# Per-chunk casts and per-chunk input loads between FFN2 and the second layer norm (8 cores, sequence block with MoE)

## The chip, the cores and the metric

One Trainium2 chip, all 8 cores, each with its own sequence of 4096 tokens and no exchange between them. The metric is the device time in microseconds of the slowest core.

## The reference, cut to what matters

Each core has x of 4096 tokens x 1024 features. LN is a layer norm.

```
h  = LN(x) W_to ; a damped rotation is scanned over time ; h = out W_from
x2 = x + 0.1 h
x3 = x2 + 0.1 (gelu(LN(x2) W_ffn1 + b1) W_ffn2 + b2)
p1 = LN(x + x3)
final = sum over 8 experts of w[e] * (silu(gate) * up) down[e]^T ,  w from the top 2 of 8 router logits
out = LN(p1 + final)
```

## The kernel before

Everything is kept transposed, features on the partitions: a tile is 512 tokens (T), 1024 features are 8 chunks (KC) of 128 x 512, and a core walks over 8 tiles (NT). Float32 buffers X0 (the input x), X2 (the running sum) and ACC (the output sum) hold one tile each; BFIN0 and BFIN1 hold the bfloat16 operand of the matmuls, in turn by tile.

A tile passes these stages: LN3 of X2 (`emit_ln`, L685), FFN1 (`emit_ffn1`, L610, 256 matmuls of L625), FFN2 (`emit_ffn2`, L639), the second layer norm p1 (`emit_ln` with twopass, L691), the router (L699 to L732), the experts (L770 gate and up, L810 down). LN1, the scan and W_from of the next tile (`make_chain`) are woven into the experts of this one.

FFN2 has two halves, `fr` = 0 and 1, each for four output chunks. A half takes four slabs (`kr`) of 1 MB of w2, with 32 matmuls of 128x512 each (L658), summed in four PSUM banks that begin with a bias matmul (L655). When a bank is done, DVE makes X2 = X2 + 0.1 PB (L668) and u = X0 + X2, in place in X2 (L671). The u of chunks 0 to 3 comes at the end of the first half, that of 4 to 7 at the end of the second.

`emit_ln` casts the eight chunks to bfloat16 on ACT (L385), sums them over the partitions on PE with a matrix of ones (L390), squares them on ACT (L393), sums again (L398); DVE then makes mean and 1/sqrt (L403 to L411) and the normalised chunks (L418, L419).

The order of the work is written out by hand: every engine has one list of instructions, filled in the order in which the Python code calls `opi` and `opd`, and `w(engine, marks)` puts a wait on a semaphore into that list. Whatever stands behind a wait on an engine is held by it. All loads and stores are issued by SP ("sync"), so they share one list.

Weights come through RING, four slots of 1 MB. `emit_slab_load` (L360) takes the next slot, makes SP wait for the matmuls that last read it, and issues one load (L369) from a bfloat16 scratch copy in HBM (scr_w, scr_gu, scr_dp). In tile 0 the copy doesn't exist yet: `prepass_unit` (L248) loads a slab in float32 into two slots by eight DMAs (L257), casts the halves on DVE (L288) and ACT (L286) into a third slot, and stores that to the scratch (L292).

The input of the next tile is loaded into X0 by `emit_xload` (L307): one wait, then eight loads of 256 KB (L312). It is called behind FFN2:

```
if i + 1 < NT:
    emit_xload(i + 1, extra=u_ms[KC - 1])
```

The output of a tile is normalised and stored (L824 to L832) in the middle of the next tile's FFN1, behind its fourth slab.

Of the kernel before, what the change touches and what calls it, by code (L numbers as in the profile page):

```python
# [14 lines left out]
T = 512  # L15
NT = S // T
KC = D // 128
# [12 lines left out]
def build(stop_stage="full"):  # L30
# [28 lines left out]
    def sb(name, shape, dt=F32):  # L59
        return es.enter_context(nc.sbuf_tensor(name, shape, dt))  # L60
# [4 lines left out]
    with es:  # L65
        X0 = sb("X0", [128, KC * T])
# [50 lines left out]
        def w(eng, ms):  # L117
            if ms is None:
                return
            if isinstance(ms, list):  # L120
                for m in ms:
                    w(eng, m)
                return
            sk, v = ms
            q[eng].append(lambda E, s=sems[sk], vv=v: E.wait_ge(s, vv))
# [8 lines left out]
        def opi(eng, sk, fn):  # L134
            cnt[sk] += STEP[sk]
            v = cnt[sk]
            q[eng].append(lambda E, fn=fn, s=sems[sk], st=STEP[sk]: fn(E).then_inc(s, st))
            if eng in DRAIN_ENGS:
                q[eng].append(lambda E: E.drain())  # L139
            return (sk, v)  # L140

        def opd(eng, sk, fn):
            cnt[sk] += STEP[sk]
            v = cnt[sk]
            q[eng].append(lambda E, fn=fn, s=sems[sk], st=STEP[sk]: fn(E).then_inc(s, st))
            return (sk, v)
# [4 lines left out]
        def xc(buf, k, width=T):  # L151
            return buf[:, k * width:(k + 1) * width]
# [12 lines left out]
        def ring_set_free(j, ms):  # L165
            if isinstance(ring_free[j], list):
                ring_free[j] = ring_free[j] + [ms]
            else:
                ring_free[j] = ms
# [133 lines left out]
        xTr = xT.rearrange("(k p) t -> k p t", p=128)  # L303
        outTr = outT.rearrange("(k p) t -> k p t", p=128)
        x_ms = [None] * (NT + 1)

        def emit_xload(i, extra=None):  # L307
            t0 = i * T
            w("sync", extra)
            ms = None  # L310
            for k in range(KC):
                ms = opd("sync", "SX", lambda E, k=k, t0=t0: E.dma_start(out=xc(X0, k), in_=xTr[k, :, t0:t0 + T]))  # L312
            x_ms[i] = ms
# [46 lines left out]
        def emit_slab_load(dram_ap, key):  # L360
            if key not in scr_ready:
                srcs, dram = _scr_srcs(key)
                ms_cs, mw, jo, oslot = prepass_unit(srcs, dst_dram=dram)
                scr_ready[key] = mw
                ring_free[jo] = [mw]
                return jo, oslot, ms_cs
            jj, slot, msf = ring_slot()
            w("sync", msf)
            ms = slot_dma(jj, lambda E, d=slot, s=dram_ap: E.dma_start(out=d, in_=s))  # L369
            return jj, slot, ms  # L370
# [3 lines left out]
        def emit_ln(src, bfin_p, gv=None, bv=None, dstf=None, out_bf=True,  # L374
                    src_ready=None, extra_swait=None, extra_twait=None, extra_vwait=None,
                    twopass=False):
            BFIN = BFINS[bfin_p]
            w("scalar", src_ready)
            w("scalar", extra_swait)
            w("scalar", bfin_user[bfin_p])  # L380
            cast_ms = [None] * KC
            sq_ms = [None] * KC
            mmS_ms = [None] * KC
            for k in range(KC):
                cast_ms[k] = opi("scalar", "S", lambda E, k=k: E.activation(out=xc(BFIN, k), in_=src(k), func=AF.Copy))  # L385
            w("tensor", bank_free[0])
            w("tensor", extra_twait)
# [251 lines left out]
        def emit_ffn2(i, g_ms, u_ms):  # L639
            x3_ms = [None] * KC  # L640
            if i == 0:
                w("tensor", ms_b2c)
            for fr in range(2):
                for kr in range(4):
                    jj, slot, msl = emit_slab_load(scr_w2[fr * 4 + kr], ("w2", fr * 4 + kr))
                    w("tensor", msl)
                    for jx in range(8):
                        w("tensor", g_ms[kr * 8 + jx])
                    mm_last = None
                    for oc4 in range(4):  # L650
                        oc = fr * 4 + oc4
                        b = 2 + oc4
                        if kr == 0:
                            w("tensor", bank_free[b])
                            opi("tensor", "T", lambda E, b=b, oc=oc: E.matmul(  # L655
                                PB[b][:], B2R[0:1, oc * 128:(oc + 1) * 128], ONER[:], start=True, stop=False))
                        for jx in range(8):
                            mm_last = opi("tensor", "T", lambda E, jx=jx, kr=kr, oc4=oc4, b=b, slot=slot: E.matmul(  # L658
                                PB[b][:], slot[:, jx * 512 + oc4 * 128: jx * 512 + (oc4 + 1) * 128], xc(G, kr * 8 + jx),
                                start=False, stop=(kr == 3 and jx == 7)))  # L660
                        if kr == 3:
                            bank_ready[b] = mm_last
                    ring_set_free(jj, mm_last)
                for oc4 in range(4):
                    oc = fr * 4 + oc4
                    b = 2 + oc4
                    w("vector", bank_ready[b])
                    x3_ms[oc] = opi("vector", "V", lambda E, oc=oc, b=b: E.scalar_tensor_tensor(  # L668
                        out=xc(X2, oc), in0=PB[b][:], scalar=0.1, in1=xc(X2, oc), op0=OP.mult, op1=OP.add))
                    bank_free[b] = x3_ms[oc]  # L670
                    u_ms[oc] = opi("vector", "V", lambda E, oc=oc: E.tensor_tensor(  # L671
                        out=xc(X2, oc), in0=xc(X0, oc), in1=xc(X2, oc), op=OP.add))
            return x3_ms

        last_gu_mm = [None]
        prev_out_so = [None]
# [5 lines left out]
        for i in range(NT):  # L682
            t0 = i * T
            x2_last = st["x2_7"]
            ms_ln3, _, _, ln3_bf, _ = emit_ln(lambda k: xc(X2, k), i % 2, gv=G3V, bv=B3V, src_ready=x2_last)  # L685
            g_ms = emit_ffn1(i, ms_ln3, ln3_bf)
            u_ms = [None] * KC
            x3_ms = emit_ffn2(i, g_ms, u_ms)
            if i + 1 < NT:
                emit_xload(i + 1, extra=u_ms[KC - 1])  # L690
            ms_p1bf, ms_p1f, ms_p1sq, p1_bf, p1_f = emit_ln(lambda k: xc(X2, k), i % 2, dstf=lambda k: xc(ACC, k), out_bf=True,  # L691
                                                            src_ready=u_ms[KC - 1], extra_vwait=prev_out_so[0], twopass=True)
            st["x2_free"] = ms_p1sq
            BFIN = BFINS[i % 2]
            w("tensor", bank_free[6])
# [53 lines left out]
            for e in range(NE):  # L749
# [48 lines left out]
                for fr in range(2):  # L798
# [5 lines left out]
                    for oc4 in range(4):  # L804
                        oc = fr * 4 + oc4
# [18 lines left out]
            def make_p2(i=i, t0=t0, acc_ms=list(acc_ms), gu_ms=last_gu_mm[0]):  # L824
                def p2():
                    _, ms_out, _, _, _ = emit_ln(lambda k: xc(ACC, k), i % 2, dstf=lambda k: xc(ACC, k), out_bf=False,
                                                 src_ready=acc_ms[KC - 1], extra_swait=gu_ms)
                    w("sync", ms_out)
                    for k in range(KC):
                        opd("sync", "SO", lambda E, k=k, t0=t0: E.dma_start(out=outTr[k, :, t0:t0 + T], in_=xc(ACC, k)))  # L830
                    prev_out_so[0] = ("SO", cnt["SO"])
                return p2  # L832
# [21 lines left out]
def _get_nc(stop_stage):  # L854
    if stop_stage not in _CACHE:
        _CACHE[stop_stage] = build(stop_stage)
    return _CACHE[stop_stage]
# [37 lines left out]
```

## Time and profile before

| what | value |
|---|---|
| median of 2 runs | 5834.64 us |
| the two runs | 5725.51 and 5943.76 us |
| the profiled execution, its own time | 5557.22 us |
| its span, slowest core (core 1) | 5555.6 us |
| spans of all 8 cores | 5534.1 to 5555.6 us |
| mean granted TensorE clock | 0.871 to 0.876 of full |

The profile is one execution; its times are not those of the two runs, which both took longer. Busy times and starts are in us from the span's start. PE is TensorE, DVE VectorE, ACT ScalarE, POOL GpSimd; SPq is SP's queue that issues DMAs. A bracket at the end of a timeline row gives the engine's idle time before it and what released it.

### The profile page before, as it was taken

To read this page: it belongs to the slowest core of one execution; us is meant where nothing else is said; L and a number is where in the kernel's file an instruction comes from. 1 tells how busy PE (TensorE), PEld (TensorE's weight loads), DVE (VectorE), ACT (ScalarE), POOL (GpSimd) and SP (SyncE) were. 2 spreads that over 40 slices of the span, in tenths; PEclk is the share of its full clock that TensorE was granted. 3 is DMA by queue.
4 is the path that set the end of the run, shared out by engine and by line. 5 is a ranking of instruction groups with operands and counts; after the bars stand their busy time and mean duration, and the time that the engine had idled before them with its cause. 6 is when DMAs were issued, how large, how long until landed. Compare 5 with 4: busy or idle time off the path is not lost.

```text
span 5555.6 us, 55775 instructions; the slowest of 8 cores (5534.1 to 5555.6 us)
## 1 busy us (share of the span) xinstructions
PE 4182.1 (75%) x17824; PEld 1772.5 (32%) x17824; DVE 1982.1 (36%) x2879; ACT 1040.6 (19%) x1559; POOL 467.2 (8%) x391
## 2 busy tenths in 40 slices
PE   1475656657898678966898678976899678976897
PEld 0122222223343233422333233432344233432343
DVE  4313432232443235332443235332443235332333
ACT  1222212221201221121211221121201211121111
POOL 0001000000200011100201010100201010100210
PEclk6687788768999889988999789988999789988999
DMA  2275657624233223314333233414234233323342
GB/s 62 91 250 174 212 201 238 230 92 147 107 128 129 99 106 114 137 61 151 107 123 136 91 107 114 137 68 151 99 122 144 84 108 113 137 75 136 114 144 91
DMA packets 178009, 712.61 MB, mean 128 GB/s; under 512 B 28609, under 2 KB 28737, under 8 KB 112194
## 3 DMA queue, kind: packets, MB, share of 16 engines
q1 hardware_dynamic: 168770, 708.95, 36.6%
q8 instruction: 156, 2.56, 0.2%
q10 hardware_dynamic: 8960, 0.10, 0.1%
q14 instruction: 123, 1.01, 0.1%
HBM read 625.09 MB, written 83.89 MB: 128 GB/s over the span
## 4 chain that ended last, share of the span: by engine, by line
PE 62%; DVE 17%; DMA 6%; ACT 5%; SPq 5%; issue 3%; DVEq 1%; ACTq 1%
PE PB L770 27%; PE PB L810 15%; PE PB L625 8%; PE PB L658 7%; SPq L257 4%; DMA RING<-guT 3%; ACT RING L286 2%; DVE ZS L438 2%; DVE PB L411 1%; ACT BFIN L385 1%; PE PB L390 1%; DVE UPE L783 1%; PE PB L598 1%; DVEq L139 1%; DVE PRD L789 1%
## 5 line engine op out<-in xcount | busy, mean ns | idle before, releaser
L770 PE MATMUL PB<-BFIN,RING 128*128 128x512 bf16 x8192 | 1877.3, 392 | 173.1 <-ACT RING L286 116.0
L770 PEld LDWEIGHTS PB<-BFIN,RING 128*128 128x128 bf16 x8192 | 814.5, 100 | 1216.5 <-issue 329.1
L810 PE MATMUL PB<-PRD,RING 128*128 128x512 bf16 x4096 | 963.9, 398 | 225.6 <-DVE PRD L789 140.0
L625 PE MATMUL PB<-BFIN,RING 128*128 128x512 bf16 x2048 | 518.9, 416 | 424.5 <-DMA RING<-scr_w 220.8
L783 DVE TENSOR_TENSOR UPE<-PB,CBE 128x512 f32<-128x512 f32 x512 | 354.2, 692 | 1024.4 <-PE PB L770 994.6
L810 PEld LDWEIGHTS PB<-PRD,RING 128*128 128x128 bf16 x4096 | 410.6, 102 | 773.7 <-issue 350.7
L816 DVE TENSOR_TENSOR ACC<-PB,ACC 128x512 f32<-128x512 f32 x512 | 354.2, 692 | 682.7 <-PE PB L810 673.6
L789 POOL TENSOR_TENSOR PRD<-SG,UPE 128x512 bf16<-128x512 bf16 x256 | 297.0, 1160 | 2879.0 <-DVE UPE L783 2804.4
L777 ACT ACTIVATE SG<-PB 128x512 bf16<-128x512 f32 x512 | 303.7, 598 | 1023.6 <-PE PB L770 1015.0
L658 PE MATMUL PB<-G,RING 128*128 128x512 bf16 x2048 | 465.0, 386 | 24.5 <-issue 14.0
L625 PEld LDWEIGHTS PB<-BFIN,RING 128*128 128x128 bf16 x2048 | 213.0, 104 | 729.0 <-issue 539.5
L658 PEld LDWEIGHTS PB<-G,RING 128*128 128x128 bf16 x2048 | 197.2, 99 | 275.3 <-issue 56.1
L668 DVE SCALAR_TENSOR_TENSOR X<-PB,X 128x512 f32<-128x512 f32 x64 | 44.3, 692 | 651.1 <-PE PB L658 651.1
L427 POOL TENSOR_TENSOR ACC<-X,MEANT 128x512 f32<-128x512 f32 x64 | 82.9, 1296 | 2056.3 <-DVE BFIN L419 2056.3
L755 ACT ACTIVATE CBE<-PB 128x512 f32<-128x512 f32 x64 | 38.2, 597 | 1142.1 <-PE PB L752 1095.4
L631 ACT ACTIVATE G<-PB,BHV 128x512 bf16<-128x512 f32 x256 | 175.7, 687 | 280.6 <-PE PB L625 280.4
L789 DVE TENSOR_TENSOR PRD<-SG,UPE 128x512 bf16<-128x512 bf16 x256 | 187.4, 732 | 62.0 <-DVE UPE L783 61.4
L286 ACT ACTIVATE RING<-RING 128x2048 bf16<-128x2048 f32 x64 | 122.2, 1909 | 383.5 <-DMA RING<-dpT 165.0
L288 DVE CAST RING<-RING 128x2048 bf16<-128x2048 f32 x64 | 80.0, 1251 | 293.9 <-DMA RING<-guT 106.4
L385 ACT ACTIVATE BFIN<-X 128x512 bf16<-128x512 f32 x128 | 68.1, 616 | 480.2 <-DVE X L671 428.4
L390 PE MATMUL PB<-BFIN,ONESB 128*128 128x512 bf16 x192 | 74.2, 556 | 95.5 <-ACT BFIN L385 95.5
L403 DVE TENSOR_SCALAR MEANT<-PB 128x512 f32<-128x512 f32 x24 | 16.6, 691 | 357.5 <-PE PB L390 357.5
(120 smaller groups left out, 1837.7 us busy)
## 6 DMA issues: line engine op xcount, KB each, us to landing
RING<-scr_gu SPq DMA_DIRECT2D x224, 1024.0 KB, 4.9
RING<-scr_w SPq DMA_DIRECT2D x112, 1024.0 KB, 5.2
RING<-scr_dp SPq DMA_DIRECT2D x112, 1024.0 KB, 5.0
RING<-guT SPq DMA_DIRECT2D x256, 256.0 KB, 5.7
scr_gu<-RING SPq DMA_DIRECT2D x32, 1024.0 KB, 4.9
RING<-dpT SPq DMA_DIRECT2D x128, 256.0 KB, 5.3
X<-xT SPq DMA_DIRECT2D x64, 256.0 KB, 5.1
RING<-w1T SPq DMA_DIRECT2D x64, 256.0 KB, 6.2
```

The source lines that it names most:

```text
L257: ms_rd = slot_dma(jj, lambda E, d=slot.bitcast(F32)[:, gg * gc_:(gg + 1) * gc_], s=srcs[hv][gg]: E.dma_start(out=d, in_=s))
L286: ms_c = opi(eng, sk, lambda E, d=dstap, s=slot.bitcast(F32)[:, 0:ncols]: E.activation(out=d, in_=s, func=AF.Copy))
L390: mmS_ms[k] = opi("tensor", "T", lambda E, k=k: E.matmul(PB[0][:], ONESB[:], xc(BFIN, k), start=(k == 0), stop=(k == KC - 1)))
L625: mmm = opi("tensor", "T", lambda E, k=k, fc4=fc4, b=b, slot=slot: E.matmul(PB[b][:], slot[:, k * 512 + fc4 * 128: k * 512 + (fc4 + 1) * 1 ...
L631: g_ms[fc] = opi("scalar", "S", lambda E, b=b, fc=fc: E.activation(out=xc(G, fc), in_=PB[b][:], func=AF.Gelu, bias=BHV[:, fc:fc + 1]))
L658: mm_last = opi("tensor", "T", lambda E, jx=jx, kr=kr, oc4=oc4, b=b, slot=slot: E.matmul(PB[b][:], slot[:, jx * 512 + oc4 * 128: jx * 512 ...
L770: mmm = opi("tensor", "T", lambda E, k=k, fc4=fc4, b=b, slot=slot, BFIN=BFIN: E.matmul(PB[b][:], slot[:, k * 512 + fc4 * 128: k * 512 + (f ...
L777: sg_ms[gc] = opi("scalar", "S", lambda E, b=b, gc=gc: E.activation(out=xc(SG, gc), in_=PB[b][:], func=AF.Silu))
L783: ms_up = opi("vector", "V", lambda E, b=b, par=par: E.tensor_tensor(out=xc(UPE, par), in0=PB[b][:], in1=CBE[:], op=OP.mult))
L789: prev_upe[par] = opi(peng, psem, lambda E, uc=uc, par=par: E.tensor_tensor(out=xc(PRD, uc), in0=xc(SG, uc), in1=xc(UPE, par), op=OP.mult))
L810: mmm = opi("tensor", "T", lambda E, k=k, oc4=oc4, b=b, slot=slot: E.matmul(PB[b][:], slot[:, k * 512 + oc4 * 128: k * 512 + (oc4 + 1) * 1 ...
L816: acc_ms[oc] = opi("vector", "V", lambda E, oc=oc, b=b: E.tensor_tensor(out=xc(ACC, oc), in0=PB[b][:], in1=xc(ACC, oc), op=OP.add))
```

## The change

It does two things. `emit_ln` takes a list of eight marks as `src_ready` and puts one wait before each cast instead of one before all; the second layer norm passes the eight u marks. And the call of `emit_xload` behind FFN2 goes; `emit_ffn2` itself issues the load of one chunk of the next tile's x right behind the u of that chunk. The first call of `emit_ln` (LN3) and tile 0's first x load stay.

```
-            w("scalar", src_ready)
+            per_chunk = isinstance(src_ready, list) and len(src_ready) == KC
+            if not per_chunk:
+                w("scalar", src_ready)
...
             for k in range(KC):
+                if per_chunk:
+                    w("scalar", src_ready[k])
                 cast_ms[k] = opi("scalar", "S", ...)
...
                     u_ms[oc] = opi("vector", "V", lambda E, oc=oc: E.tensor_tensor(
                         out=xc(X2, oc), in0=xc(X0, oc), in1=xc(X2, oc), op=OP.add))
+                    if i + 1 < NT:
+                        w("sync", u_ms[oc])
+                        x_ms[i + 1] = opd("sync", "SX", lambda E, oc=oc, t1=(i + 1) * T: E.dma_start(
+                            out=xc(X0, oc), in_=xTr[oc, :, t1:t1 + T]))
...
-            if i + 1 < NT:
-                emit_xload(i + 1, extra=u_ms[KC - 1])
             ms_p1bf, ms_p1f, ms_p1sq, p1_bf, p1_f = emit_ln(...
-                                                            src_ready=u_ms[KC - 1], extra_vwait=prev_out_so[0], twopass=True)
+                                                            src_ready=u_ms, extra_vwait=prev_out_so[0], twopass=True)
```

SP's list from FFN1 to the first expert of a tile behind the first, before (scr_w1 and scr_w2 are the scratch copies of the FFN weights, scr_gu that of gate and up):

```order
L830 DMA outT<-ACC 128x512 x7
L369 DMA RING<-scr_w1 128x4096 [waits sem_T] x4
L369 DMA RING<-scr_w2 128x4096 [waits sem_T] x8
L312 DMA X0<-xT 128x512 [waits sem_V]
L312 DMA X0<-xT 128x512 x7
L369 DMA RING<-scr_gu 128x4096 [waits sem_T] x4
```

The same stretch of SP's list now:

```order
L836 DMA outT<-ACC 128x512 x7
L369 DMA RING<-scr_w1 128x4096 [waits sem_T] x4
L369 DMA RING<-scr_w2 128x4096 [waits sem_T] x4
L679 DMA X0<-xT 128x512 [waits sem_V] x4
L369 DMA RING<-scr_w2 128x4096 [waits sem_T] x4
L679 DMA X0<-xT 128x512 [waits sem_V] x4
L369 DMA RING<-scr_gu 128x4096 [waits sem_T] x4
```

Four x loads, each with a wait for DVE, have moved ahead of the last four w2 loads.

ACT's list behind FFN2 of tile 1, before (L385 are the casts, L393 the squares, L409 the square root):

```order
L385 ACTIVATE BFIN1<-X2 128x512 [waits sem_V,sem_T]
L385 ACTIVATE BFIN1<-X2 128x512 x7
L393 ACTIVATE BFIN1<-X2 128x512 [waits sem_T] x8
L409 ACTIVATE PB1<-PB1 128x512 [waits sem_V]
```

And now:

```order
L389 ACTIVATE BFIN1<-X2 128x512 [waits sem_T,sem_V]
L389 ACTIVATE BFIN1<-X2 128x512 [waits sem_V] x7
L397 ACTIVATE BFIN1<-X2 128x512 [waits sem_T] x8
L413 ACTIVATE PB1<-PB1 128x512 [waits sem_V]
```

No instruction has changed its place there; seven casts have a wait of their own.

## Rows read from the trace of the kernel before

**Rows 1.** The page's head and part 1: busy time, share, instructions.
```profile
span 5555.6 us, 55775 instructions; the slowest of 8 cores (5534.1 to 5555.6 us)
PE 4182.1 (75%) x17824; PEld 1772.5 (32%) x17824; DVE 1982.1 (36%) x2879; ACT 1040.6 (19%) x1559; POOL 467.2 (8%) x391
```

**Rows 2.** The page's part 4, the chain that ended last, by engine and line.
```profile
PE 62%; DVE 17%; DMA 6%; ACT 5%; SPq 5%; issue 3%; DVEq 1%; ACTq 1%
PE PB L770 27%; PE PB L810 15%; PE PB L625 8%; PE PB L658 7%; SPq L257 4%; DMA RING<-guT 3%; ACT RING L286 2%; DVE ZS L438 2%; DVE PB L411 1%; ACT BFIN L385 1%; PE PB L390 1%; DVE UPE L783 1%; PE PB L598 1%; DVEq L139 1%; DVE PRD L789 1%
```

**Rows 3.** Timeline (start, us, instruction), tile 3, end of FFN2 and second LN.
```profile
2605.29 0.69 DVE L671 TENSOR_TENSOR X<-X 128x512 f32<-128x512 f32 x1
2606.06 3.69 SPq L312 DMA_DIRECT2D X<-xT  x8
2606.13 4.26 ACT L385 ACTIVATE BFIN<-X 128x512 bf16<-128x512 f32 x8 [59.59 <-DVE X L671]
2610.54 3.57 PE L390 MATMUL PB<-BFIN,ONESB 128*128 128x512 bf16 x8 [6.14 <-ACT BFIN L385]
2613.91 2.48 PE L398 MATMUL PB<-BFIN,ONESB 128*128 128x512 bf16 x8
```

**Rows 4.** Timeline, tile 3, middle of FFN2.
```profile
2545.83 29.64 SPq L369 DMA_DIRECT2D RING<-scr_w  x5
...
2575.01 0.39 PE L655 MATMUL PB<-ONER,B2R 1*128 1x512 bf16 x1
...
2575.97 0.69 DVE L671 TENSOR_TENSOR X<-X 128x512 f32<-128x512 f32 x1
```

**Rows 5.** DMA issues (count, KB each, us to landing): 2553.0 to 2555.5, 2561 to 2562, 2575 to 2576.
```profile
RING<-scr_w SPq DMA_DIRECT2D x1, 1024.0 KB, 4.9
RING<-scr_w SPq DMA_DIRECT2D x1, 1024.0 KB, 5.3
RING<-scr_w SPq DMA_DIRECT2D x1, 1024.0 KB, 4.7
```

**Rows 6.** Timeline of PE and ACT, tile 4, sums of LN3.
```profile
3040.09 1.89 PE L390 MATMUL PB<-BFIN,ONESB 128*128 128x512 bf16 x8
3041.81 3.53 PE L398 MATMUL PB<-BFIN,ONESB 128*128 128x512 bf16 x8
```

**Rows 7.** Timeline, tile 3, FFN1 behind the output stores; landing of its first slab.
```profile
2505.64 4.45 SPq L830 DMA_DIRECT2D outT<-ACC  x8
2510.19 65.28 SPq L369 DMA_DIRECT2D RING<-scr_w  x12
2516.49 29.27 PE L625 MATMUL PB<-BFIN,RING 128*128 128x512 bf16 x128 [30.45 <-DMA RING<-scr_w]
...
RING<-scr_w SPq DMA_DIRECT2D x1, 1024.0 KB, 6.1
```

**Rows 8.** Windows: stretch, us, busy of each engine, PEclk, DMA share, GB/s.
```profile
2513.00:2516.50 3.50, 0.01 (x1) 0.04 (x2) 0.00 (x0) 0.00 (x0) 0.00 (x0) 0.50 1.02 396
2516.50:2519.00 2.50, 2.50 (x6) 0.83 (x7) 0.00 (x0) 0.00 (x0) 0.00 (x0) 0.50 1.03 341
2519.00:2522.00 3.00, 3.00 (x14) 1.37 (x13) 0.00 (x0) 2.05 (x3) 0.00 (x0) 0.91 0.99 407
2546.00:2575.00 29.00, 29.00 (x132) 12.48 (x131) 4.15 (x6) 0.54 (x1) 0.00 (x0) 1.00 0.41 145
2575.00:2604.00 29.00, 29.00 (x132) 12.57 (x132) 5.28 (x8) 0.00 (x0) 0.00 (x0) 1.00 0.11 37
2646.00:2700.00 54.00, 50.51 (x222) 21.67 (x221) 16.63 (x23) 14.89 (x26) 22.59 (x18) 0.97 0.31 107
```

**Rows 9.** Timeline of PE: after 5.53 us of idle, undisturbed, and tile 7's FFN1.
```profile
2736.63 9.40 PE L810 MATMUL PB<-PRD,RING 128*128 128x512 bf16 x32 [5.53 <-DVE PRD L789]
2747.60 7.07 PE L810 MATMUL PB<-PRD,RING 128*128 128x512 bf16 x32
2907.74 27.80 PE L770 MATMUL PB<-BFIN,RING 128*128 128x512 bf16 x128
5029.25 30.68 PE L625 MATMUL PB<-BFIN,RING 128*128 128x512 bf16 x128 [30.92 <-DMA RING<-scr_w]
```

**Rows 10.** Timeline, tile 0, middle of FFN2: fifth slab's float32 loads, cast, last u.
```profile
368.84 4.62 SPq L257 DMA_DIRECT2D RING<-w2T  x8
378.58 0.69 DVE L671 TENSOR_TENSOR X<-X 128x512 f32<-128x512 f32 x1
378.93 1.91 ACT L286 ACTIVATE RING<-RING 128x2048 bf16<-128x2048 f32 x1 [10.98 <-DMA RING<-w2T]
```

## The prediction

> **What bounds the kernel now.** I read the page's head and its groups first. PE is busy 75% of the span and no other engine more than 36% [rows 1]. The chain that ended last runs for 62% of the span through PE, and two MoE lines, L770 and L810, hold 42% of it; the lines that this change can touch (L385, L390, the w2 slabs behind L658) hold 1 to 7% each [rows 2]. So only those moments count in which PE stands still around FFN2, and I read these from the timeline of tile 3, one of six tiles (1 to 6) that repeat one pattern.
>
> At the end of FFN2 the chain goes from engine to engine [rows 3]: DVE ends the last u (L671) at 2605.29 + 0.69 = 2605.98, ACT starts the eight casts at 2606.13 and needs 4.26 us for all, and PE, idle for 6.14 us, starts the sums at 2610.54. The casts run 0.533 us apart (4.26 / 8), though only the last of the eight chunks is new at 2605.98; chunks 0 to 3 have been ready since 2576.66, half an FFN2 earlier [rows 4]. That is slack the change can take.
>
> In the middle of FFN2 PE doesn't stop at all [rows 4]: the second half begins at 2575.01, right behind the first. The reason is the queue of SP: five w2 slab loads are issued from 2545.83 on, each as soon as PE frees a ring slot, so the first slab of the second half has long been there. A landing takes 4.7 to 5.3 us [rows 5]; PE eats a slab in 32 matmuls, 6.9 us (a quarter of the 27.80 us of 128, [rows 9]).
>
> **The change, part by part.**
>
> Early casts. Before, ACT's eight casts waited for u of chunk 7. Now each waits for its own chunk. Chunks 0 to 3 are cast in the middle of FFN2, 4 to 6 while DVE makes the next u (a pair of L668 and L671 takes 1.72 us, a cast 0.61), and one cast is left behind the last u. PE waits for the last cast still. Its start comes at 2605.98 + 0.15 + 0.61 + 0.14 = 2606.88 instead of 2610.54: 3.66 us gained. PE then idles 2.5 us instead of 6.14. In tile 3 the granted clock is low around this place and the two rounds of sums take from 2610.54 to 2613.91 + 2.48 = 2616.39, 5.85 us [rows 3]. Where they follow on PE's work with no gap, L390 runs at 1.89 us for eight and both rounds take 3040.09 to 3045.34, 5.25 us [rows 6]. So 0.6 us more may be gained, and I take it: 4.26 us a tile, bounds 3.66, with no clock gained, and 4.9, with twice as much. Eight tiles: 8 x 4.26 = 34 us (29 to 39). Nothing is behind it that would absorb this: MEANT, the reciprocal, the router, all follow on PE's sums one after the other.
>
> The x loads in SP's queue. This is where it costs. SP's order shows eight w2 loads in a row before; now four, then four x loads that wait for DVE, then four w2 loads. u of chunk 3 can't exist before PE has ended the first half: so no slab of the second half can be asked for before that, where until now all were asked for ahead. SP holds everything behind a wait: at the LN output of the previous tile, the same trap already stands in the kernel. There SP waits for DVE, issues eight output stores and only then, at 2510.19, the FFN1 slab; PE had been idle 30.45 us and starts at 2516.49 [rows 7].
>
> The Trainium skill says why there is no way round it (DMA: Bandwidth & Descriptors, "Anatomy of one DMA"): a semaphore wait is made on the issuing sequencer before the transfer is dispatched, and the DMA engines wait for nothing. The 30.45 us agree with that.
>
> The new stall, from tile 3's rows: u of chunk 3 ends at 2575.97 + 0.69 = 2576.66; SP issues that x load at 2576.74 and, an x issue taking 3.69 / 8 = 0.46 us [rows 3], the slab at 2577.20. Landing: alone 4.9 us [rows 5]; 6.1 us with 2 MB of stores issued just ahead and three slabs behind [rows 7]. Here 256 KB stand ahead, at 396 GB/s 0.66 us [rows 8], so I take 4.9 + 0.6 = 5.5 us, plus 0.2 us to PE. PE starts at 2582.9 instead of 2575.01: 7.9 us (7.1 to 8.5). The three slabs behind it come 2.6 us apart at that rate, and PE wants one in 6.9: no second stall.
>
> By the skill's fit of one DMA, 2.0 us and its bytes over 436 GB/s (same page and section, stated for the GpSimd path), slab and x chunk would be there in 5.0 us instead of 5.5: an estimate 0.5 us shorter a tile, 3 us in all. The measured 4.9 us for the slab alone, against 4.4 by that fit, speaks for my figure.
>
> A stall of this length also costs clock. After 5.53 us of idle, 32 matmuls took 9.40 us where the next 32 took 7.07, at the full 2.4 GHz: 2.3 us lost; after 30.45 us, 128 took 29.27 against 27.80: 1.5 us lost; the first 2.5 us of that run stand at 0.50, which is 1.2 GHz [rows 7 to 9]. I take 2.3 us (1.5 to 3, the last from the 30.68 us of tile 7's 128, [rows 9]). The second half runs 28 us behind it at 1.00 [rows 8], so the clock is back when it ends. Sum for a tile of 1 to 6: 7.9 + 2.3 = 10.2 us lost (8.6 to 11.5), less 4.26: +5.9 us. Six: +36 us.
>
> Tile 0 makes its w2 slabs from float32: SP issues the loads of the fifth slab at 368.84, 4.62 us for eight, and ACT casts them 5.47 us after the last issue, at 378.93 [rows 10]. Now they wait for u of chunk 3 (378.58 + 0.69 = 379.27), the x load's 0.46 us, and go out from 379.8 to 384.4: 10.9 us later, and the clock, low already, adds nothing. Slabs of this tile are 13 us apart, so nothing is caught up. Less 4.26: +6.7 us. Tile 7 loads no x: -4.3 us.
>
> The other half of the x loads stands where all eight stood, behind the last u and ahead of the MoE slabs. Those are wanted 40 us later, where the MoE stretch of rows 8 begins at 2646, and LN and router hide them either way: cost zero, and if that cover were gone the 3.69 us of issues a tile [rows 3]. X0 is filled earlier, but the next tile's LN1 casts it only after expert 0's first matmuls: no gain.
>
> Sum: 36 + 6.7 - 4.3 = +38 us (with the bounds of gain and loss +24 to +51). On the profiled execution, 5557.2 us with a span of 5555.6, that is 5595 us, +0.7%. The two runs shown took 5725.51 and 5943.76, both above the profiled one, their median 5834.64; with the same 38 us: 5873 us.
>
> **The rivals.**
> (a) The x loads cost nothing: SP's stop is covered because the slabs' landing is short against PE's 28 us of matmuls. For it: DMA moves 145 GB/s in the first half of FFN2 and 37 in the second [rows 8], so there is room. Against it: all four slots are freed only by PE's matmuls of the first half, and the issue, not the rate, is late. Then the casts' gain stands alone: 5834.6 - 34 = 5801 us, faster than before. Chance 0.07.
> (b) The supply is slow, and becomes the bound of the second half. All eight cores ask for 4 MB and x at the same moment. If a slab takes t us, a landing alone is 2.3 us and t (4.9 less 1.05 MB at 396 GB/s), so the last of the four lands at 2577.2 + 2.3 + 4.25 t, and PE ends 6.9 us later instead of at 2604.4 (2610.54 - 6.14): the half grows by 4.25 t - 18.0 us. It decides, with 2% of 5834.6 (117 us) as the mark, from t = 9.2 us, 113 GB/s. Rows show 107 GB/s as a mean of a MoE stretch [rows 8]: t = 9.8, 23.7 + 2.3 - 4.3 = 21.7 a tile, 130 + 2.4 = 132 us, so 5967 us. Against it: 396 and 407 GB/s in the stretch where four slabs really were queued on all cores [rows 8]. Chance 0.05.
> (c) The change doesn't gain what it should: casts 0 to 6 are early but PE's start is held by something else (the first matmul of the sums waits for its bank too, freed long before by LN3, so I see nothing). Then 34 us are missing: 5834.6 + 72 = 5907 us. Chance 0.08.
>
> **How the numbers follow.** My own case has 0.80, and is the predicted time, 5873 us. The mechanism alone would give 5859 to 5886. The runs before differ by 218 us, though, and the profiled execution lies at 5557: the time after can come out anywhere between 5557 + 38 and 5944 + 38, which gives the range 5590 to 5985; it holds (a), (c) and (b) too. A measurement of this kernel can tell about 2% from no change. My case, (a) and (c) lie inside that, so within 2%: 0.86; slower by over 2%: (b) and the spread of the runs, 0.11; faster by over 2% only by that spread, 0.03.
>
> **What would show it.** Right: in tiles 1 to 6 PE idles 7 to 9 us ahead of the second half's first bias matmul (L655 before, L659 now), released by a w2 DMA; the first slab of it is issued some 0.5 us after u of chunk 3; the granted clock dips behind it; PE's idle ahead of the sums of the second LN falls from 6.14 to about 2.5 us, in all eight tiles; tile 7 has no stall. Wrong: no PE idle in the middle of FFN2 (then (a)); several stalls in one half (then (b)); 6 us ahead of the sums as before (then (c)). A time below 5780 in a comparison with 5835 would say that the casts are worth more than I made them.

## The result

| | before | changed |
|---|---|---|
| median of the timed runs | 5643.45 us (14 runs) | 5720.88 us (16 runs) |
| lowest of them | 5551.49 us | 5603.92 us |
| ratio, changed to before | | 1.0094, 95% interval 1.0058 to 1.013 |
| span of the profiled execution, slowest core | 5555.6 us | 5607.3 us |
| mean of its eight cores | 5544.3 us | 5589.5 us |

The kernel is 0.94% slower, some 52 us, and the two profiles, taken as means of their eight cores, differ by 45 us. The medians of all runs lie 77 us apart and scatter by more than the effect, because in many executions one die runs at a lower clock; every ratio here leaves such executions out, and of a profile that fell into one only the undisturbed cores are used, which the text names.

The page's head and the chain of the changed kernel:

```profile
span 5607.3 us, 55880 instructions; the slowest of 8 cores (5576.5 to 5607.3 us)
PE 4189.3 (75%) x17824; PEld 1770.4 (32%) x17824; DVE 1982.0 (35%) x2879; ACT 1046.3 (19%) x1559; POOL 467.1 (8%) x391
PE 62%; DVE 17%; DMA 7%; ACT 5%; SPq 4%; issue 4%; DVEq 1%; ACTq 1%; POOL 0%; POOLq 0%
PE PB L776 27%; PE PB L816 14%; PE PB L629 8%; PE PB L662 8%; SPq L257 4%; DMA RING<-guT 3%; ACT RING L286 2%; DMA RING<-scr_w 2%; DVE ZS L442 2%; DVE PB L415 1%; DVE UPE L789 1%; PE PB L394 1%; PE PB L602 1%; DVE PRD L795 1%; DVEq L139 1%
```

Against [rows 1, 2] two things have moved the way of the loss: L662, FFN2's matmuls, has 8% of the chain instead of 7%, and `DMA RING<-scr_w`, PE's wait for a slab of w1 or w2, has come up to 2%. That is the loss, seen in the coarsest view. The finer one is the timeline of tile 3 (core 3), FFN2's middle, to be held against [rows 4] (columns: start, us, instruction, idle before and its releaser):

```profile
2572.90 1.90 PE L662 MATMUL PB<-G,RING 128*128 128x512 bf16 x8
...
2598.45 5.51 SPq L679 DMA_DIRECT2D X<-xT  x4
2602.86 0.69 DVE L675 TENSOR_TENSOR X<-X 128x512 f32<-128x512 f32 x1
2603.65 0.63 ACT L389 ACTIVATE BFIN<-X 128x512 bf16<-128x512 f32 x1 [1.10 <-DVE X L675]
2604.05 2.10 SPq L369 DMA_DIRECT2D RING<-scr_w  x4
2610.85 0.58 PE L659 MATMUL PB<-ONER,B2R 1*128 1x512 bf16 x1 [8.88 <-issue]
2611.36 3.59 PE L662 MATMUL PB<-G,RING 128*128 128x512 bf16 x8
2619.80 22.62 PE L662 MATMUL PB<-G,RING 128*128 128x512 bf16 x104
```

The u of chunk 3 ends at 2602.86 + 0.69 = 2603.55, the last of the four x loads waits for it, and the four slab loads of half 2 all leave at 2604.05 or later, behind that load. PE stands still for 8.88 us, and its first eight matmuls take 3.59 us where the first eight of half 1 took 1.90: the clock has fallen. Two landings of that moment, of the fourth x chunk and of the first slab:

```profile
X<-xT SPq DMA_DIRECT2D x1, 256.0 KB, 3.4
RING<-scr_w SPq DMA_DIRECT2D x1, 1024.0 KB, 5.7
```

And the windows of the same place (us, busy of PE, PEld, DVE, ACT, POOL, PEclk, DMA share, GB/s): half 1, the stall, three stretches of half 2.

```profile
2572.00:2602.00 30.00, 29.97 (x136) 12.63 (x133) 4.15 (x6) 2.02 (x4) 0.00 (x0) 1.00 0.15 49
2602.00:2610.80 8.80, 0.00 (x0) 0.00 (x0) 1.39 (x2) 1.18 (x2) 0.00 (x0) 0.69 0.80 292
2610.80:2613.50 2.70, 2.65 (x7) 0.86 (x8) 0.00 (x0) 0.00 (x0) 0.00 (x0) 0.50 1.01 428
2613.50:2617.50 4.00, 4.00 (x14) 1.18 (x12) 0.00 (x0) 0.00 (x0) 0.00 (x0) 0.74 0.66 279
2617.50:2642.00 24.50, 24.50 (x113) 10.88 (x113) 3.88 (x6) 1.26 (x2) 0.00 (x0) 1.00 0.06 13
```

In [rows 8] the DMA engines moved 145 GB/s during half 1 and 37 during half 2. Now they move 49 in half 1, then 292, 428 and 279 while PE waits and starts again, then 13: the four slabs of half 2, and 1 MB of x with them, asked for together and too late.

The gain is there as well, at the second norm (the last cast, then the sums; compare [rows 3]):

```profile
2644.09 0.63 ACT L389 ACTIVATE BFIN<-X 128x512 bf16<-128x512 f32 x1 [1.09 <-DVE X L675]
2644.87 1.89 PE L394 MATMUL PB<-BFIN,ONESB 128*128 128x512 bf16 x8 [2.45 <-ACT BFIN L389]
2646.59 3.54 PE L402 MATMUL PB<-BFIN,ONESB 128*128 128x512 bf16 x8
```

PE idles 2.45 us instead of 6.14, and the sums start at the full clock.

From such timelines each tile can be cut into stages: S, the first sum of LN3; F, the first bias matmul of FFN2; the end of half 1; H, the fifth bias matmul; the end of half 2; P, the first sum of the second norm; M, the first matmul behind the router (L752 before). "Idle to P" runs from the end of half 2 to P, "experts" from M to the next tile's S. The table gives changed minus before, each the mean of eight cores, in us.

```
tile   LN3+FFN1  half 1  gap 1-2  half 2  idle to P   P to M  experts    sum
0         2.34    0.27    10.23   -0.59     -3.69     -0.50    -1.35     6.70
1        -1.99    0.00    10.54    2.41     -3.69     -1.12     1.59     7.74
2         1.09    0.00     9.25    2.33     -3.69     -0.80    -0.08     8.10
3        -1.33    0.00     8.93    2.18     -3.69     -1.07     0.50     5.52
4        -0.03    0.00     8.91    2.37     -3.69     -0.77     0.45     7.23
5        -0.08    0.00     8.85    2.19     -3.69     -1.14     0.78     6.91
6         0.79    0.00     8.84    2.49     -3.69     -1.08     0.46     7.82
7         0.13    0.00     0.00    0.00     -3.69     -1.06     0.43    -4.19
all       0.93    0.27    65.56   13.38    -29.53     -7.54     2.78    45.84
```

Tile 7 loads no next x, has no gap, and keeps the gain alone.

### The profile page after: what moved, and what is told of

The parts are those of the page before. It is cut to its first block, busy times and chain, and to the rows that moved or that the text cites. A ratio compares the mean times of both kernels' runs of the same rounds, so it can differ in the third digit from the quotient of the medians.

```text
span 5607.3 us, 55880 instructions; the slowest of 8 cores (5576.5 to 5607.3 us)
## 1 busy us (share of the span) xinstructions
PE 4189.3 (75%) x17824; PEld 1770.4 (32%) x17824; DVE 1982.0 (35%) x2879; ACT 1046.3 (19%) x1559; POOL 467.1 (8%) x391
## 4 chain that ended last, share of the span: by engine, by line
PE 62%; DVE 17%; DMA 7%; ACT 5%; SPq 4%; issue 4%; DVEq 1%; ACTq 1%; POOL 0%; POOLq 0%
PE PB L776 27%; PE PB L816 14%; PE PB L629 8%; PE PB L662 8%; SPq L257 4%; DMA RING<-guT 3%; ACT RING L286 2%; DMA RING<-scr_w 2%; DVE ZS L442 2%; DVE PB L415 1%; DVE UPE L789 1%; PE PB L394 1%; PE PB L602 1%; DVE PRD L795 1%; DVEq L139 1%
## 5 line engine op out<-in xcount | busy, mean ns | idle before, releaser
L662 PE MATMUL PB<-G,RING 128*128 128x512 bf16 x2048 | 484.9, 397 | 18.5 <-issue 8.3
L672 DVE SCALAR_TENSOR_TENSOR X<-PB,X 128x512 f32<-128x512 f32 x64 | 44.3, 692 | 725.9 <-PE PB L662 725.9
L662 PEld LDWEIGHTS PB<-G,RING 128*128 128x128 bf16 x2048 | 201.3, 101 | 284.8 <-issue 84.0
L709 PE MATMUL PB<-RT,BFIN 128*128 128x8 bf16 x256 | 15.8, 167 | 155.7 <-DVE BFIN L423 155.7
```

## The experiments

Two theories of the loss stood against each other. Order: the slab loads of half 2 stand behind SP's wait for DVE and are asked for too late. Traffic: 1 MB of x beside FFN2's slabs is what PE waits for. The first two kernels do one part of the change each.

**Casts alone.** x loads back in one piece behind the last u; the new casts kept.

```
-                    if i + 1 < NT:
-                        w("sync", u_ms[oc])
-                        x_ms[i + 1] = opd("sync", "SX", ...)
...
             x3_ms = emit_ffn2(i, g_ms, u_ms)
+            if i + 1 < NT:
+                emit_xload(i + 1, extra=u_ms[KC - 1])
```

Expected:

> Casts per chunk, x loads where they were (all eight behind the last u). Both theories of the loss say the same here: no stall in the middle of FFN2, PE's idle ahead of the second norm's sums 2.45 us instead of 6.14, sums some 1 us shorter. So 8 x (3.69 + 0.95) = 37 us less than before, ratio 0.993. Rival: the casts' gain is taken back further on (PE reaches the router earlier but waits there), then 0.

Measured by stage (cores 0 to 3 against the same cores of before): gap and half 2 as before (-0.1 and -0.2 us over all tiles), idle to P -29.5, P to M -7.3, experts +11.9, of it expert 0 +9.4; spans 23 us shorter. The timed ratio is 0.9991, 0.9969 to 1.0014. So the gain is what it should be at its place, 37 us, but the whole kernel doesn't show it: the expected 0.993 is outside the interval. Something behind the router takes part of it back; see the control below. The metric hides some more: in the executions that the ratio counts, the mean of the eight cores is 14 us below before and the slowest core only 5, because the cores end within 46 us of each other on average instead of 29. Why they spread is not shown.

**x loads alone.** The changed kernel with `src_ready=u_ms[KC - 1]`, all casts behind the last u.

> x loads per chunk, casts all behind the last u as before. If the two parts simply add: gap of 8.9 us in the middle of FFN2 in tiles 1 to 6, half 2 longer by 2.3 us, tile 0 later by 10 us, no gain at the sums: 46 + 37 = 83 us more than before, ratio 1.015. Rival: the parts act on each other (early casts on ACT are needed for, or hide behind, the stall): clearly away from 83.

Measured: gap +65.5 us, half 2 +14.0, idle to P 0.0, P to M -2.4, LN3 and FFN1 +3.7, experts +0.1, eight-core mean 81 us above before (expected 83). The -2.4 at the sums was not expected, since the casts are as late as before, and why it is there was not followed up. The timed ratio is 1.012, 1.0091 to 1.0149, whose upper end is just below the 1.015 expected. From FFN2 to the router the parts add within some 2 us: 76.8 us for this part and -37.0 for the casts (803.5 against 840.5 us on the same four cores of before) make 40, and the changed kernel has 42. What is left over is P to M: each part alone shortens the same sums, by 2.4 and 7.3 us, and both together by 7.5.

**x loads behind the slabs.** x loads 0 to 3 keep their waits, but stand in SP's list behind the four slab loads of half 2.

```
+                if fr == 1 and i + 1 < NT:
+                    for oc in range(4):
+                        w("sync", u_ms[oc])
+                        opd("sync", "SX", ...)      # x chunk oc
                 for oc4 in range(4):
...
-                    if i + 1 < NT:
+                    if fr == 1 and i + 1 < NT:
```

> The changed kernel with x loads 0 to 3 moved in SP's list behind the four slab loads of half 2; casts early. Theory order (the slab loads are asked for too late because they stand behind SP's wait for DVE): gap in the middle 0, 37 us less than before, ratio 0.993. Theory traffic (1 MB of x beside FFN2's slabs is what PE waits for): a gap or stalls inside half 2 of several us remain, ratio 1.00 or above.

Tile 3 on core 1:

```profile
2536.49 7.23 SPq L369 DMA_DIRECT2D RING<-scr_w  x2
2543.81 2.02 SPq L671 DMA_DIRECT2D X<-xT  x4
2543.26 0.39 PE L659 MATMUL PB<-ONER,B2R 1*128 1x512 bf16 x1
2543.57 1.90 PE L662 MATMUL PB<-G,RING 128*128 128x512 bf16 x8
...
2575.09 1.89 PE L394 MATMUL PB<-BFIN,ONESB 128*128 128x512 bf16 x8 [2.45 <-ACT BFIN L389]
```

The x loads run inside FFN2's second half, 0.5 us behind its start, and PE has neither gap nor stall. The gap in tiles 1 to 6 is 0.0 in all cores. The mean of the cores is 29 us below before, a second profile gives 23.6 (expected 37). Four timed runs gave no ratio; the two lowest, 5526.38 and 5539.70 us, lie 0.5% below the mean of the eight lowest of before in the same session, where 0.7% was expected. A second timing is told below. Order is shown, for the gap; traffic is refuted as its cause.

**The wait without the transfer.** SP waits for u 0 to 3 between the slabs of the two halves as in the changed kernel, but issues nothing there; the four x loads follow behind the slabs of half 2. To x loads behind the slabs this adds:

```
+                    elif i + 1 < NT:
+                        w("sync", u_ms[oc])
```

> SP keeps the four waits for u 0 to 3 between the w2 slabs of the two halves, but the four x transfers go behind the slabs of half 2. Theory order: the gap stays, shorter only by the issue and the bytes of the last x chunk: 8.0 us of 8.9, half 2 still 2.3 us longer. Theory traffic: gap gone.

Tile 3, core 3:

```profile
2593.68 0.69 DVE L680 TENSOR_TENSOR X<-X 128x512 f32<-128x512 f32 x1
2594.50 1.95 SPq L369 DMA_DIRECT2D RING<-scr_w  x4
2596.54 1.95 SPq L671 DMA_DIRECT2D X<-xT  x4
2600.47 0.58 PE L659 MATMUL PB<-ONER,B2R 1*128 1x512 bf16 x1 [7.68 <-issue]
2600.98 3.59 PE L662 MATMUL PB<-G,RING 128*128 128x512 bf16 x8
```

Over tiles 1 to 6 and cores 0 to 3 the gap is 8.5 us on average, against 9.0 on the same cores of the changed kernel, and half 2 is 2.5 us longer than before. So the wait by itself makes about 95% of the gap. The 0.9 us that the missing transfer was expected to save came out as 0.5: the slab is issued 1.71 us behind PE's end instead of 2.07, and its landing is hardly shorter.

**x loads on ACT.** The mirror image: transfers and moments as in the changed kernel, but ACT issues each behind the cast of its chunk, and SP waits for nothing in FFN2.

```
                 cast_ms[k] = opi("scalar", "S", ...)
+                if per_chunk and xnext is not None:
+                    x_ms[xnext] = opd("scalar", "SX", ...)      # x chunk k
```

> x loads per chunk as in the changed kernel, but issued by ACT, each behind the cast of the same chunk, so SP waits for nothing in FFN2. Bytes and moments of the transfers are those of the changed kernel. Theory order: gap in the middle 0, 37 us less than before, less what seven issues of 0.1 to 0.4 us on ACT ahead of the sums' squares cost (at most 3 us in all). Theory traffic: gap and stalls in half 2 like those of the changed kernel.

```profile
2570.28 0.34 ACTq L391 DMA_DIRECT2D X<-xT  x1
2573.74 0.37 ACTq L391 DMA_DIRECT2D X<-xT  x1
2573.70 0.39 PE L662 MATMUL PB<-ONER,B2R 1*128 1x512 bf16 x1
2605.54 1.89 PE L397 MATMUL PB<-BFIN,ONESB 128*128 128x512 bf16 x8 [2.45 <-ACT BFIN L389]
```

No gap, with the transfers at the same moments of FFN2. P to M is 7.2 us shorter than before over all tiles, against 7.3 with the casts alone, so ACT's issues cost nothing that can be seen. The mean of the cores is 16 us below before: the gain again falls short of 37. Expert 0 takes 7.5 of the missing 21 us; the rest lies in other experts and in LN3 and FFN1 and is no larger than the scatter between two executions of one kernel (15 us, see the controls).

**No repeated waits.** In the changed kernel PE starts about 1.1 us behind the landing of the slab it waits for. PE's list has nine waits between: one for the slab, eight for gelu marks, which in half 2 repeat those of half 1.

```
                     for jx in range(8):
-                        w("tensor", g_ms[kr * 8 + jx])
+                        if fr == 0:
+                            w("tensor", g_ms[kr * 8 + jx])
```

> The changed kernel; PE's 32 waits for the gelu marks are put out in half 2 only, where half 1 has already waited for the same ones. In the changed kernel PE starts 1.13 us behind the landing of the slab (2609.72 to 2610.85), in the FFN1 stall of before 0.2 us. Theory: PE's sequencer goes through nine waits between the slab's semaphore and the matmul, about 0.1 us each: gap 8.1 us instead of 8.9, whole kernel 6 us less than the changed one. Rival: the 1.1 us belong to the semaphore or the cold start of the PE: gap stays 8.9.

The gap can be cut at the slab's issue and landing, tiles 1 to 6, all cores. In the changed kernel: 2.07 to 2.08 us from PE's end to the issue in every case, 5.2 to 9.8 us landing with a mean of 6.0 and a median of 5.5, 1.09 to 1.18 us from landing to PE. Without the repeated waits the last part is 0.24 to 0.25 us in all 48 cases, so 0.87 us belong to the eight waits. The gap only fell from 9.2 to 8.6, where 0.8 less was expected, since the slabs landed 0.3 us later in this execution, and the whole kernel didn't get shorter (mean of the cores 5603.4 against 5589.5 us): the term is shown, its gain is lost in the scatter between executions. With the waits gone the profile also names the releaser, which had been "issue":

```profile
2594.47 0.58 PE L660 MATMUL PB<-ONER,B2R 1*128 1x512 bf16 x1 [7.79 <-DMA RING<-scr_w]
```

**Controls.** Both kernels profiled a second time.

> The kernel before, profiled a second time as a control for the table by stage. In the profiles with early casts the first 128 gate-up matmuls behind the router have 10 to 15 slow steps (over 0.35 us from one start to the next) in most tiles, in those of before and of x loads only 8 to 10, and expert 0 takes 1 to 1.5 us longer. If that belongs to the early casts, this profile shows 8 to 10 again; if it is the day or the chip, 10 to 15.

> The changed kernel again, on the chip of the other runs of this call. Parts of the stall: 2.07 us from PE's end to the issue of the slab, 5.2 to 6 us landing, 1.1 us to PE; sums as in the first profile: middle gap +65 us over the tiles, half 2 +13, idle ahead of the sums -29.5. Rival: the landing of 5.2 to 9.8 us was peculiar to that execution, then the gap differs by over 1 us a tile.

The second profile of the changed kernel repeats the first: gap +64.7 us, half 2 +13.0, idle to P -29.5, P to M -7.5. Its slabs landed in 5.2 to 8.1 us, mean 5.8, so landings far above 5.3 us were not peculiar to one execution. The control of before has none of these (0.3, 0.2, 0.0, -0.3). Its span mean is 15 us above the first all the same, nearly all in tile 0 and in the experts of one tile: this is the scatter between two executions of one kernel, and differences of whole spans below it mean nothing. For the stages the controls are sharp. The slow steps repeat too: in tiles 1 to 6 the first 128 gate-up matmuls have 9.6 of them on average in both profiles of before, and 10.8 to 13.5 in every profile with early casts, so they belong to the early casts. Us per core, tiles 0 to 7 together (FFN2 to router is F to M):

```
profile                      FFN2 to router   expert 0
before                            841.2         441.2
before again                      843.2         442.9
x loads alone                     918.0         441.5
changed                           883.3         447.0
changed again (cores 0 to 5)      882.0         448.5
casts alone (cores 0 to 3)        803.5         450.2
x loads behind the slabs          803.4         453.1
the same, second profile          804.2         451.0
x loads on ACT                    804.4         448.6
```

Whatever has early casts spends 6 to 12 us more in expert 0, and what hasn't stays within 2 us. The kernels not in the table agree: 7 us more with the wait without the transfer (cores 0 to 3), 9 with no repeated waits, 16 with stores later (below). The timelines show where. The kernel before (core 1), then the one with x loads behind the slabs (core 1), tile 3, from the router on:

```profile
2645.77 29.49 PE L770 MATMUL PB<-BFIN,RING 128*128 128x512 bf16 x128
2678.03 7.07 PE L810 MATMUL PB<-PRD,RING 128*128 128x512 bf16 x32 [2.78 <-DVE PRD L789]
```

```profile
2609.54 30.43 PE L781 MATMUL PB<-BFIN,RING 128*128 128x512 bf16 x128
2642.75 8.47 PE L821 MATMUL PB<-PRD,RING 128*128 128x512 bf16 x32 [2.78 <-DVE PRD L800]
```

The same matmuls, the same wait of 2.78 us between them, and 0.94 and 1.40 us more. The windows around that wait, of before and of the experiment:

```profile
2674.20:2681.20 7.00, 4.22 (x20) 1.79 (x19) 3.20 (x4) 0.00 (x0) 6.05 (x5) 1.00 0.42 152
```

```profile
2638.00:2645.00 7.00, 4.22 (x16) 1.58 (x14) 3.12 (x4) 0.00 (x0) 5.14 (x5) 0.80 0.43 152
```

PE is busy for the same 4.22 us, but gets 16 matmuls started instead of 20: the granted clock is 0.80 there instead of 1.00. This is no single place: over expert 0 of all tiles and cores PE is idle for 44.4 us before and 44.3 in this kernel, while the mean granted clock is 0.940 and 0.913. So the give-back is clock. From P to M it is the other way round, 0.55 before and 0.61 with early casts. That early casts bring both is shown by the table's nine profiles, six with them and three without; why the clock comes back later behind the router when PE's pause in front of the sums is shorter stays open.

**Timed again, x loads behind the slabs.**

> The run behind_slabs again, for an interval. By stage it lost 28.5 us against before, not 37: -29.5 idle ahead of the sums and -7.5 behind them, but +8.6 in the experts. Theory (the gain is partly given back by a slower clock behind the router): ratio 0.994 to 0.996. Rival (that was scatter): 0.993.

The six runs gave no ratio with an interval. The two lowest, 5544.70 and 5545.55 us, stand against 5554.33 to 5568.82 for the four lowest of before in the same session, about 0.3% below; in the first session it was 0.5%. Both are less than the 0.7% without a give-back, which speaks for the give-back, but four runs don't decide it.

**Stores later.** The trap of this change has an older twin in the kernel, [rows 7]: SP waits in the middle of FFN1 for the last tile's norm, and PE idles for 31 us in each of tiles 1 to 7. To x loads behind the slabs this kernel adds one thing: the eight output stores and their wait are issued behind the fourth w2 slab of half 1 instead of in FFN1 (those of the last tile excepted).

```
-                    w("sync", ms_out)
-                    for k in range(KC):
-                        opd("sync", "SO", ...)
+                    pending_stores[0] = stores      # the same nine steps
...
+                if fr == 0 and pending_stores[0] is not None:
+                    pending_stores[0]()
+                    pending_stores[0] = None
                 if fr == 1 and i + 1 < NT:
```

> As the run behind_slabs, and the eight output stores with SP's wait for the last tile's norm, until now behind FFN1's fourth slab, issued behind the fourth w2 slab of FFN2's first half. Theory order: PE's idle of 31 us in the middle of FFN1 (tiles 1 to 7) ends with ACT's gelu instead of with the slab, at about 8 to 12 us; 7 x 20 = 140 us less, with the 37 us 177 us less than before, ratio 0.968. Theory traffic, or PE waits there for something else as well: the idle stays near 31 us and the ratio near 0.993.

```profile
2409.49 3.08 PE L402 MATMUL PB<-BFIN,ONESB 128*128 128x512 bf16 x8
2412.41 27.79 PE L629 MATMUL PB<-BFIN,RING 128*128 128x512 bf16 x128
2440.69 5.97 SPq L846 DMA_DIRECT2D outT<-ACC  x8
```

The 30.45 us in front of FFN1's second half are gone altogether, not down to 8 or 12: PE goes from the sums straight on, so its four banks, which gelu frees, were free each time it wanted one. With them goes the slow start, 27.79 us for 128 instead of 29.27. LN3 and FFN1 take 234 us less over the eight tiles, the mean of the cores is 246 us below before, and expert 0 gives back 16 of them. Timed: 0.9547, 0.9488 to 0.9606, against 0.968 expected.

> The run stores_later again, for a tighter interval: its stages gave 246 us less than before, of them 234 in LN3 and FFN1. Ratio 0.956.

Again 0.9573, with 0.9544 to 0.9601: a version 4.3% faster than the kernel before, and more against the changed one. Of all the runs this is the only one in which the order of SP's list was worth more than 2%.

## Why the prediction was right or wrong

The step that failed is the last one, from the sum to the verdict. My sum gave 38 us, +0.7%; I then wrote that a measurement can tell "about 2%" from no change, and put 0.86 on "within 2%". The measurement told 0.94% with an interval of 0.36% to either side, so it is a slowdown and not a tie. The mark of 2% came from two runs 218 us apart; the interval of the comparison is five times narrower. The predicted 5873 us hung on that same pair: the median of 14 runs of before is 5643, not 5835, and that 5721 lies in my range of 5590 to 5985 says little, since that range is as wide as the scatter of the pair.

In the sum itself the mechanism was right, with one exception behind the router, and one term was mis-sized, the new stall: 7.9 us a tile predicted, 9.2 measured.

Term by term, predicted and measured over all tiles:

| term | predicted | measured |
|---|---|---|
| gap in FFN2, tiles 1 to 6 | 6 x 7.9 = 47.4 | 55.3 |
| clock behind it | 6 x 2.3 = 13.8 | 14.0 |
| tile 0 | 10.9 | 9.9 (10.23 + 0.27 - 0.59) |
| idle in front of the sums | -8 x 3.66 = -29.3 | -29.5 |
| sums and what follows, to the router | -8 x 0.6 = -4.8 | -7.5 |
| experts | 0 | +2.8, of it expert 0 +5.8 |
| LN3 and FFN1 | 0 | +0.9 |
| sum | +38 | +46 |

- The new stall: I put "4.9 + 0.6 = 5.5 us, plus 0.2 us to PE". The landing took 6.0 on average, the median being the 5.5 predicted and the rest a tail up to 9.8, and the way from landing to matmul 1.1. The 0.2 us had been read from the FFN1 stall of [rows 7], where PE's list holds no such row of waits behind the slab's; in FFN2 eight gelu waits stand there, which cost nothing to be seen before the change, when PE passed from half 1 to half 2 without a gap. The step to the issue, 2.2 us, measured 2.07.
- Clock after the stall: 2.3 us taken from a pause of 5.53 us, 2.3 measured per tile. The pause here was 8.9 us, and my other row, a pause of 30.45 us, had cost 1.5, so the match is in part luck.
- Early casts: 3.66 us predicted, 3.69 measured in every tile; PE's remaining idle 2.5 predicted, 2.45 measured. From the sums to the router 0.5 to 1.1 us instead of 0.6, -7.5 in all instead of -4.8. That doesn't all need early casts: x loads alone have -2.4.
- "Nothing is behind it that would absorb this" was wrong in part: expert 0 gives back 6 to 12 us through the clock when casts are early, 5.8 in the changed kernel's profile. I had put the experts at nothing from the order of the work alone, without a look at the clock there.
- Tile 0 went as argued, "nothing is caught up". The second four x loads of each tile cost nothing that the stages show (experts +0.1 us in x loads alone). The granted clock in tile 0 is 0.84 at this place in the kernel before (370 to 378 us, core 1), not as low as I wrote, but half 2 got no longer (-0.59).
- Rival (a), x loads cost nothing, would have been right for the transfers and wrong for the wait: with the slabs ahead of the wait the gap is 0. Rival (b), slow supply, never came: 428 GB/s in the first stretch behind the stall, one gap per tile. That all eight cores ask at the same moment, as I wrote, no trace shows, since each core counts from its own start. Rival (c) is refuted at its place and has a little truth behind the router.
- The Trainium skill's fit for one DMA (DMA: Bandwidth & Descriptors, "Anatomy of one DMA", stated for the GpSimd path) would have made the landing 5.0 us, an estimate; measured 5.2 to 9.8. By the same section of the Trainium skill a semaphore wait is made on the issuing sequencer before the transfer is dispatched. The runs agree: the gap is there in the four kernels in which the wait stands ahead of the slabs (changed, x loads alone, the wait without the transfer, no repeated waits), with or without the transfers there, and in none of the others.
- "No way round it" held for this order of the list alone: with the x loads behind the slabs or issued by ACT the gap is 0.0.

## What to carry to other kernels

A load that must wait for compute should not stand in an issuing engine's list ahead of loads that need not: read the list of the queue, not the moment at which the data become free, and issue the prefetches first or the waiting loads from an engine that has just waited for the same thing. Cutting a wait into pieces helps the consumer (here ACT and PE) and harms the queue that carries it, so the two must be judged apart. Before tuning a stall of 4 us, look for the same pattern elsewhere in the same list: here its twin cost eight times as much.

## What was not expected of the hardware

- 0.87 us for eight semaphore waits on PE that were already satisfied, 0.11 us each. Where PE didn't stand still, as at the same place in the kernel before, they cost nothing to be seen.
- The landing of one 1 MB slab at the same place of the program took 5.2 us on some cores and up to 9.8 us on others of the same execution (median of 48: 5.5), without any difference in their programs. Why is not shown.
- The granted clock behind a pause depends on more than the pause: the same 2.78 us wait in expert 0 cost nothing in the kernel before and 1.40 us with early casts, 1.00 against 0.80 granted.
- Two executions of the kernel before differed by 15 us in the mean of their spans, 13 of them in tile 0 and 4 in the experts of tile 5.
